# A mixture-of-experts block whose expert tiles are scattered with adding transfers instead of gathered at the end

## The reference

```
logits = x @ router_w + router_b
topv, topi = jax.lax.top_k(logits, 2)
topw = jax.nn.softmax(topv, axis=-1)
comb = einsum('bsk,bske->bse', topw, onehot)
h1 = einsum('bsd,edf->ebsf', x, W1) + b1[:, None, None, :]
h2 = einsum('bsd,edf->ebsf', x, W2) + b2[:, None, None, :]
h = h2 * jax.nn.silu(h1)
eo = einsum('ebsf,efd->ebsd', h, W3) + b3[:, None, None, :]
return einsum('bse,ebsd->bsd', comb, eo)
```

## Time and profile before

| what | value |
|---|---|
| median of three runs | 258.11 us (257.36 to 258.13) |
| profiled execution, its own time | 257.8 us |
| its span | 255.9 us |
| attentions, up to the last transpose of `xm` | 0 to 139 us |
| routing | 139 to 158 us |
| expert loop | 160 to 224 us |
| final gathers, sum and norm | 224 to 256 us |
| PE busy, DVE busy, POOL busy | 72%, 71%, 47% |

### The profile page before, as it was taken

How to read it: one execution, slowest core, us unless ns; L and a number is a source line. 1 busy time by engine, 2 the same in 40 slices (tenths; PEclk the granted TensorE clock), 3 DMA queues, 4 the chain that set the end, 5 groups by cost and what they waited for, 6 DMA issues and landing times. The chain is left out here.

```text
span 255.9 us, 7235 instructions
## 1 busy us (share of the span) xinstructions
PE 183.2 (72%) x2412; PEld 161.5 (63%) x2413; DVE 182.7 (71%) x428; ACT 118.8 (46%) x385; POOL 119.5 (47%) x220
## 2 busy tenths in 40 slices
PE   0477999999999998988774421899999999900000
PEld 0365878788887877777563421899998999900000
DVE  6406799999999999989973496277676777705344
ACT  2344868878788777676242110244454544400000
POOL 0315346655688778744225203445453341047771
PEclk9997999999999999999998555599999999975555
DMA  7699900000008000000001000011112232011212
GB/s 229 147 352 385 289 16 4 3 1 5 1 3 235 18 3 3 1 13 14 23 14 31 0 0 21 23 42 41 62 52 50 41 62 41 21 41 51 51 41 82
DMA packets 21337, 16.06 MB, mean 63 GB/s; under 512 B 3032, under 2 KB 18464, under 8 KB 21312
## 3 DMA queue, kind: packets, MB, share of 16 engines
q1 hardware_dynamic: 19248, 12.02, 16.0%
q0 software_dynamic: 1344, 2.76, 5.2%
q10 hardware_dynamic: 720, 0.95, 1.2%
HBM read 11.78 MB, written 3.93 MB: 61 GB/s over the span
## 5 line engine op out<-in xcount | busy, mean ns | idle before, releaser
L476 POOL DMA_INDIRECT early<-xm_scratch,tok_i x26 | 26.3, 1012 | 44.2 <-DMA early<-xm_scratch,tok_i 26.7
L898 DVE TENSOR_REDUCE smax<-score 128x16 f32<-128x1024 f32 x24 | 29.0, 1209 | 11.9 <-PE score L551 11.9
L384 POOL TENSOR_TENSOR k<-kt,cst 128x512 f32<-128x512 f32 x24 | 25.3, 1054 | 16.4 <-ACT kt L772 16.4
L905 DVE TENSOR_TENSOR s_sb<-score,smax 128x1024 f32<-128x1024 f32 x24 | 29.4, 1224 | 1.6 <-PE bank L499 0.8
L782 ACT ACTIVATE pt_sb<-bank 128x512 f32<-128x512 f32 x48 | 26.2, 594 | 9.3 <-PE bank L499 8.8
L551 PE MATMUL score<-k,q 64*128 64x256 f32 x192 | 26.3, 393 | 0.0
L499 PE MATMUL bank<-cst,s_sb 128*128 128x128 f32 x192 | 25.9, 279 | 0.0
L915 DVE RECIPROCAL rsum<-bank 128x128 f32<-128x128 f32 x24 | 22.8, 951 | 2.4 <-PE bank L584 2.4
L499 PEld LDWEIGHTS bank<-cst,s_sb 128*128 128x128 f32 x192 | 22.1, 144 | 0.8 <-issue 0.7
L702 PE MATMUL bank<-w,pt_sb 128*128 x160 | 22.2, 282 | 0.0
L691 PE MATMUL score<-xgt,w_now 128*128 128x128 f32 x160 | 21.4, 291 | 0.4 <-ACT xgt L854 0.4
(11 more groups left out here) (167 smaller groups left out, 383.8 us busy)
## 6 DMA issues: line engine op xcount, KB each, us to landing
w_up<-in_L_ffn_W SPq DMA_DIRECT2D x2, 2048.0 KB, 12.1
w<-in_L_ffn_W SPq DMA_DIRECT2D x8, 256.0 KB, 6.5
y_scratch<-eo SPq DMA_DIRECT2D x1, 1536.0 KB, 7.7
y_scratch<-eo SPq DMA_DIRECT2D x10, 128.0 KB
cst<-in_consts ACTq DMA_DIRECT2D x1, 672.5 KB, 4.2
early<-in_x SPq DMA_DIRECT2D x1, 512.0 KB, 6.0
early<-in_ctx SPq DMA_DIRECT2D x1, 512.0 KB, 4.3
xm_scratch<-xm SPq DMA_DIRECT2D x8, 64.0 KB, 1.5
```

The lines of the kernel that those rows point to most:

```text
L384: g.tensor_tensor(k2[:, n % 3, :, :, :], kt[:, n % 2, :].rearrange("c (b u k) -> c b u k", b=2, u=1).to_broadcast([P, 2, NQ, S]), mask_p.r ...
L476: pool.indirect_dma_start(xg[:, j, :], None, xm_d[:, :], bass.IndirectOffsetOnAxis(ap=tok_i[:, j:j + 1], axis=0)).then_inc(g_gather, 16)
L898: v.tensor_reduce(smax[:, :, :], score[:, :, :].rearrange("q b (p k) -> q b p k", k=S), AX.X, ALU.max).then_inc(d_mx, 1)
L905: v.tensor_tensor(s_sb[:, :, :].rearrange("q b (p k) -> q (b p) k", k=S), score[:, :, :].rearrange("q b (p k) -> q (b p) k", k=S), smax[:, ...
```

## The change

The gate weights move ahead of the scatter. DVE splits the weights of the two experts into three bf16 parts, multiplies them with the one-hot matrix (`hi_g`), and PE turns them round with 16 more matmuls, so that each slot has its weight (`g_slot`). `keep_out` multiplies by it. The destination of a slot is its token's row (`row_i`), and a spare row per partition for an empty slot. POOL scatters each tile with an indirect DMA that adds into one of two tables, the even tile of a pair into `y_scratch_a`, which starts as `base`, the odd one into `y_scratch_b`, which starts as zero. A scatter waits until the one before it into the same table has landed. The first seven pairs are scattered by unrolled code between the gathers; the others by a loop of POOL, whose sources are two reused tiles (`eo_last`, `row_now`), and DVE waits before it overwrites them. At the end SP reads both tables in plain order, and DVE adds the two.

The core of the diff (new code of the same lines left out):

```diff
+SURE = NT - 1
+NE_KEPT = 2 * SURE - 1
...
-            sp.wait_ge(y_zero, 16)
+            sp.wait_ge(c_base, NT)
+            sp.dma_start(y_d[0][0:SPARE, :].rearrange("(t q) e -> q t e", q=P), base[:, :, :]).then_inc(y_zero, 16)
+
             sp.wait_ge(d_ex, 1)
             last = sp.value_load(last_i[0:1, 0:1], min_val=NT - 1, max_val=NJ // 2 - 1)
-            with sp.Fori(0, last + 1) as i:
-                sp.wait_ge(d_eo, 2 * i + 2)
-                sp.dma_start(y_d.rearrange("(a q) e -> q a e", q=P)[:, bass.ds(i * 2, 2), :],
-                             eo[:, bass.ds(i * 2, 2), :]).then_inc(y_out_s, 16)
+            sp.wait_ge(y_zero, 64)
+            sp.wait_ge(g_sc[0], last * 16 + 16)
+            for h in range(2):
+                sp.dma_start(yg[:, 4 * h:4 * h + 4, :], y_row[0][:, 4 * h:4 * h + 4, :]).then_inc(in_ya, 16)
+            sp.wait_ge(g_sc[1], last * 16 + 16)
+            for t in range(NT):
+                sp.dma_start(yg[:, NT + t, :], y_row[1][:, t, :]).then_inc(g_yg[t], 16)
...
+            def scatter(u, idx, src):
+                pool.indirect_dma_start(y_d[u][:, :], bass.IndirectOffsetOnAxis(ap=idx, axis=0), src, None,
+                                        compute_op=ALU.add).then_inc(g_sc[u], 16)
+
+            for i in range(4):
+                gather(i)
+            pool.wait_ge(d_row, 2)
+            pool.wait_ge(y_zero, 64)
+            for i in range(SURE):
+                gather(i + 4)
+                for u in range(2):
+                    j = 2 * i + u
+                    pool.wait_ge(d_eo, j + 1)
+                    if i >= 1:
+                        pool.wait_ge(g_sc[u], 16 * i)
+                    scatter(u, row_i[:, j:j + 1], eo[:, j, :] if j < NE_KEPT else eo_last[:, u, :])
+            for i in range(SURE + 4, NG // 2):
+                gather(i)
...
-            for t in range(NT):
-                for k in range(2):
-                    pool.indirect_dma_start(yg[:, 2 * t + k, :], None, y_d[:, :],
-                                            bass.IndirectOffsetOnAxis(ap=slot_i[:, k, t:t + 1], axis=0)).then_inc(g_yg[t], 16)
-            last_scale(0, NT - 1)
-            last_scale(NT - 1, NT)
+            all_done()
+            with pool.Fori(SURE, last + 1) as i:
+                for u in range(2):
+                    pool.wait_ge(g_sc[u], 16 * i)
+                    pool.wait_ge(g_all, 2 * i + u + 1 - 2 * SURE)
+                    pool.wait_ge(d_eo, 2 * i + 1 + u)
+                    all_done()
+                    pool.wait_ge(y_zero, 64)
+                    scatter(u, row_now[:, u:u + 1], eo_last[:, u, :])
+            for k in range(3):
+                last_scale(k, 3 * k, min(3 * k + 3, NT))
...
+            gates = rv[:, 5:7, :].rearrange("q k t -> q (k t)")
+            link(v.tensor_copy(gate_p[:, 0, :], gates))
...
+            v.tensor_tensor(hi_g[:, :, :, :], hi_hot[:, :, :].rearrange("q c (u j) -> q c u j", u=1).to_broadcast(part),
+                            gate_p[:, :, :].rearrange("q r (c u) -> q c r u", u=1).to_broadcast(part),
+                            ALU.mult).then_inc(d_gp, 1)
...
                 hidden(1, 8 * i + 12)
+                if not kept:
+                    dve.wait_ge(g_sc[0], 16 * i + 16)
+                    last_row(0, 2 * i + 2)
                 dve.wait_ge(pe_e, 2 * i + 3)
-                keep_out(0, 2 * i + 2)
+                if kept:
+                    keep_out(0, 2 * i + 2)
+                else:
+                    keep_last(0, 2 * i + 2)
                 dve.wait_ge(d_hh, 8 * i + 16)
                 load_up(1, eb)
+            with dve.Fori(0, SURE - 1) as i:
+                turn_of(i, True)
+            with dve.Fori(SURE - 1, last) as i:
+                turn_of(i, False)
...
+            for t in range(NT + 2):
+                if t < NT:
+                    add_up(t)
+                if 1 <= t <= NT:
+                    spread(t - 1)
+                if t >= 2:
+                    mean_var(t - 2)
+                if t == NT:
+                    normalise(0)
+            for t in range(1, NT):
+                normalise(t)
```

More of the change, by code:

```diff
@@ L56 @@
 C_ORD = C_T + 2 * NT
-C_END = C_ORD + NE
+C_U = C_ORD + NE
+C_END = C_U + 1
+SPARE = NT * P
 def decoder_kernel(nc, t_in, consts, out):
@@ L168, in decoder_kernel @@
         tok_i = sb("tok_i", [P, NG], I32)
+        spare = sb("spare", [P, NG])
+        row_now = sb("row_now", [P, 2], I32)
+        row_i = sb("row_i", [P, NG], I32)
+        gate_r = sb("gate_r", [P, 2, 2 * NT])
+        gate_p = sb("gate_p", [P, 3, 2 * NT], BF16)
+        hi_g = sb("hi_g", [P, 2 * NT, 3, NG], BF16)
+        g_slot = sb("g_slot", [P, NG])
         xs = sb("xs", [P, 2, P])
@@ L252, in decoder_kernel @@
         y_zero = sem("y_zero")
-        y_out_s = sem("y_out_s")
+        g_sc = [sem("g_sc_a"), sem("g_sc_b")]
+        in_ya = sem("in_ya")
+        d_gate = sem("d_gate")
+        d_gp = sem("d_gp")
+        pe_gate = sem("pe_gate")
+        d_row = sem("d_row")
+        d_sum = sem("d_sum")
         g_all = sem("g_all")
@@ L267, in decoder_kernel @@
         d_fin = sem("d_fin")
[L269 to L270 removed]
+        xm_d = nc.dram_tensor("xm_scratch", (NT * P + 1, D), F32, kind="Internal").ap()
+        y_d = [nc.dram_tensor("y_scratch_" + k, (SPARE + P, D), F32, kind="Internal").ap() for k in "ab"]
         block = ctx.enter_context(nc.Block())
@@ L474, in _, with gather @@
             pool.wait_ge(d_tok, 1)
[L475 to L479, removed]
+            def gather(i):
+                if i >= 1:
+                    pool.wait_ge(g_gather, 32 * i)
+                for j in (2 * i, 2 * i + 1):
+                    pool.indirect_dma_start(xg[:, j, :], None, xm_d[:, :],
+                                            bass.IndirectOffsetOnAxis(ap=tok_i[:, j:j + 1], axis=0)).then_inc(g_gather, 16)
@@ L675, in _ @@
             k.then_inc(pe_tok, 1)
+            ps_gate = bank[6][:, 0:3 * NG]
+            pe.wait_ge(d_gp, 1)
+            for c in range(2 * NT):
+                k = mm(ps_gate, lo_hot[:, c, :], hi_g[:, c, :, :].rearrange("q r j -> q (r j)"),
+                       start=(c == 0), stop=(c == 2 * NT - 1))
+            k.then_inc(pe_gate, 1)
             ps_h1, ps_h2 = [bank[0], bank[2]], [bank[1], bank[3]]
@@ L1124, in keep_out, with last_row, keep_last @@
                 v.tensor_scalar(eo[:, bass.ds(j, 1), :].rearrange("q a e -> q (a e)"), ps_e[u][:, 0:D],
-                                0.0, None, ALU.add).then_inc(d_eo, 1)
+                                g_slot[:, bass.ds(j, 1)], None, ALU.mult).then_inc(d_eo, 1)
+            def last_row(u, j):
+                v.tensor_copy(row_now[:, u:u + 1], row_i[:, bass.ds(j, 1)]).then_inc(d_row, 1)
+            def keep_last(u, j):
+                v.tensor_scalar(eo_last[:, u, :], ps_e[u][:, 0:D], g_slot[:, bass.ds(j, 1)], None,
+                                ALU.mult).then_inc(d_eo, 1)
             dve.wait_ge(in_moe, MOE_LOADS)
@@ L1134, in _ @@
             take_slots(0)
+            slot_rows()
+            slot_gates()
+            dve.wait_ge(d_gate, 1)
             dve.wait_ge(g_gather, 64)
@@ L1150, in _, with turn_of @@
             keep_out(0, 0)
-            with dve.Fori(0, last) as i:
+            def turn_of(i, kept):
                 ea, eb = pair_of(i + 2)
@@ new lines, in add_up, with spread, mean_var @@
+            def add_up(t):
+                dve.wait_ge(in_ya, 16 * (t // 4 + 1))
+                dve.wait_ge(g_yg[t], 16)
+                v.tensor_tensor(acc[:, t, :], yg[:, t, :], yg[:, NT + t, :], ALU.add).then_inc(d_sum, 1)
+            def spread(t):
+                dve.wait_ge(d_sum, t + 1)
+                v.bn_stats(fstats[:, t, :], acc[:, t, :]).then_inc(d_st, 1)
+            def mean_var(t):
+                dve.wait_ge(d_st, 2 * NT + t + 1)
+                v.bn_aggr(fmv[:, t, :], fstats[:, t, :]).then_inc(d_fmv, 1)
@@ L1197, in _ @@
-            for n in range(NT // 2, NT):
-                normalise(n)
+            for t in range(NT + 2):
[9 more added lines that the diff above has]
+                normalise(t)
 def _consts():
```

71 lines of the change are left out of this document (41 added, 30 removed).

## The result

| what | before | after |
|---|---|---|
| median of four runs each, same chip | 257.88 us | 262.29 us (261.4 to 263.49) |
| ratio, 95% interval | | 1.0177 [1.0132, 1.0222] |
| span of the profiled execution | 255.9 | 261.5 (its own time 263.49) |
| first loop turn's `xs` | 170.94 | 172.06 |
| `xs` of turns 6, 7, 8 | 207.23, 213.09, 218.89 | 210.25, 223.16, 235.77 |

The forecast was 256.7, faster. The time lies inside the range and on the wrong side. A disturbed execution (one of the four of experiment 3's second kernel took 297.70 us) is left out of every ratio.

A forecast was written before the change was run, and what follows sets the result against it. It took the 31.7 us tail, 20 of them POOL making gather descriptors, behind a loop with PE and DVE nearly full; -12.3 + 1.3 + 0.8 + 6.3 + 2.5 = -1.4 gave 256.7 us, range 253.5 to 259.5 (250 to 264 with the cases).

The forecast's parts named there:

- 1.9 in hand: Expert loop: the scatter of tile 13 could end at 209.5, its output allows 211.4, so POOL has 1.9 us spare.
- The forecast's second case: POOL becomes the bound: an adding transfer costs it 1.31, not 0.95; 260.6 us, chance 0.21.
- The tail: Behind E, the end of the last expert tile: 31.7 us become 19.4, 12.3 shorter, bounds 10.5 to 14.
- The start: Before the loop: five linked DVE steps and `hi_g` make `xs` 1.3 us later, bounds 0.6 to 2.4.
- The loop: Expert turns: added copies cost 0.8 us in all, bounds 0 to 2; POOL's four transfers, 5.25 a turn, keep up.
- The wait in turn 7: DVE waits before filling tile 16 until the scatter of tile 14 has landed: 6.3 us, bounds 3.5 to 10.
- The clock: PE idles 5.1 us in the turn-7 wait, its clock falls: 2.5 us more, bounds 0 to 2.6.
- the first case: Short stall: the turn-7 wait is 4.1, PE idles 2.9, under the clock's 3.2, so no clock loss; 252.0 us, chance 0.24.
- The slow landing: An adding write lands in 3.15, not 2.2, costing 0.95 in stall and tail each: 258.6 us; in the forecast's 0.45.
- copies hold POOL's descriptors back: Fourth case: DVE's copies block POOL, 6.5 us a turn, scatter of tile 13 5.4 late; 262.1 us, chance 0.07.

The follow-up runs named there:

- experiment 3's second kernel: Changed kernel with all ten pairs scattered by unrolled code from tiles of their own, gathers of pairs 11 and 12 behind the last scatter: 253.06 us, ratio 0.9842.
- experiment 1: Changed kernel with plain scatters that overwrite instead of adding: 261.08 us in a single execution.
- The gates alone: Kernel before with only the gate part: weights turned round to the slots and multiplied in at the copy out of PSUM: 259.35 us, ratio 1.0064.
- experiment 6: Plain scatters on the changed kernel with trailing gathers moved (254.49 us); gates, gathers ahead, or both on the kernel before (254.47 to 259.35 us).
- timed six-pairs-ahead kernel: Kernel before with the gathers of the first six pairs fired one behind another, two gather semaphores: 255.55 us, ratio 0.9993.
- the one with gates: Kernel before with gates computed per slot and six pairs gathered ahead: 258.62 us, ratio 1.0106.
- experiment 4: Changed kernel, turn 6 without its two waits; gathers of pairs 11 and 12 between scatters 15 and 16 (258.41 us), or behind POOL's loop (253.68 us).
- experiment 2: Changed kernel with the gathers of pairs 11 and 12 moved behind POOL's loop: 254.86 us, ratio 0.9912.
- first kernel of experiment 3: Changed kernel with all ten pairs scattered by unrolled code from tiles of their own, so no tile is reused: 254.65 us, ratio 0.9912.
- plain scatters: Changed kernel with overwriting instead of adding scatters and the gathers of pairs 11 and 12 behind POOL's loop: 254.49 us, ratio 0.990.
- experiment 5: Changed kernel with more gathers ahead, two semaphores: seven pairs, no tile reuse, trailing gathers moved (262.22 us); six pairs, none trailing (259.33 us).
- second kernel of experiment 5: Changed kernel with six pairs gathered ahead without waiting for each landing, one more pair per turn, none trailing: 259.33 us, ratio 1.0054.
- first kernel of experiment 5: Changed kernel without tile reuse, gathers of pairs 11 and 12 behind the last scatter, seven pairs gathered ahead: 262.22 us, ratio 1.0217.

## Why the prediction was wrong

**The failed step** is in the paragraph on the loop: "POOL now issues four transfers per turn: 4 x (1.012 + 0.30) = 5.25 us by the mean of its gathers", and "POOL has 1.9 in hand". It took the price of a gather for an adding scatter. The scatter measured 1.66 in the mean, 1.56 with DVE idle (the one at 245.12), and without the addition 1.00 (experiment 1). So POOL had nothing in hand: its scatter of tile 13 ended at 221.38 (219.80 + 1.58) and not at 211.4. The 10.0 us are made up like this. At tile 1 POOL was 2.9 late already (180.88 for 178.0), 1.8 of it because the gathers of pair 4 started at 174.90 and not at 173.08. Its six turns took 6.75 each and not 5.25, 9.0 in all, 7.8 of it from twelve scatters at 0.65 over the mean that was taken and the rest from gathers at 1.10. The 1.9 in hand goes off that. The forecast's second case named this and its threshold, 0.14 us more per scatter, gave it a chance of 0.21, and priced it by the slowest gather, 0.36 more. With 0.65 its formula gives 14 x 0.65 - 1.9 = 7.2, beside the 5.13 + 2.26 = 7.4 of turn 6. That the two agree so well is in part luck: DVE waited there for tiles 11 and 12, and the formula leaves out the late start. The mechanism of the case was right and its size nearly a factor of two low. Its sign, scatters above 1.1 us with POOL never idle, was the one that showed. No row showed an adding write, and then the bound belongs farther out than the slowest row of another kind.

Point by point:

- *The tail, -12.3*: measured -13.5, right. Inside it two errors cancel in part. The first sum on DVE started at E + 7.8 and not 5.8, because the last scatter stood behind that of tile 18 (243.18 + 1.55) and then took 1.56. What follows took 10.4 and not 13.6: DVE takes a tile in 0.49 and not 0.85, since its three small instructions start 0.1 to 0.2 apart and their rows overlap.
- *The start, +1.3*: measured 1.1, right; `hi_g` took 1.46.
- *The loop, +0.8*: 1.9, too low and in bounds. It is two longer turns, 7.9 and 6.8 in turns 1 and 4; the kernel before has two as well (6.5 and 6.8 in turns 1 and 3). The gates alone (experiment 6) put E 1.65 later, with 2.1 from turn 0 to turn 8, and beside the timed six-pairs-ahead kernel the one with gates has turns of 5.97 for 5.83. But the kernels of experiment 4 have the weights too (copies of 0.34 instead of 0.28) and turns of 5.8. What makes single turns longer was not found.
- *The wait in turn 7, +6.3*: 6.68, the turn 6.8 longer. Shown by experiment 2, which took it away. Its parts were off by the backlog twice: tile 14 landed 16.5 after tile 13 was out, not 14.2, and DVE came to it 9.9 after and not 8.0, so that the wait came out near the forecast by luck in part.
- *The clock, +2.5*: 2.2, and the same thing in turn 6, inside its 7.05. The 3.2 us that the first case leaned on is no fixed time: the clock fell about 2.1 and 4.7 after PE's two stops.
- *Missing: the wait in turn 6, +7.05.* It is the whole miss: -1.4 + 7.05 gives 5.65, measured 5.6; the errors of the other terms, -1.2 to +1.1 each, cancel.
- *The rivals.* The short stall did not happen. POOL as the bound is what came. The slow landing did not: a scatter into `y_scratch_a` took 3.7 from issue to landing, 2.1 of it behind the generation. That copies hold POOL's descriptors back is not what made the scatters slow: with DVE idle the transfer at 245.12 took 1.56, beside copies the mean was 1.66, and the slowest of all runs 2.15 (222.31 in the first kernel of experiment 3). It is the rule of the Trainium skill, page "SBUF — State Buffer", section "SBUF: two separate sides" (the "DVE blocks DMA" trap). By that rule nearly each of two copies a turn would have added 0.7; the traces show scatters at most 0.6 above the 1.56, and 0.1 in the mean of the changed kernel.

DMA packets show what the addition changes: the queue of POOL's transfers moved 1,344 packets before, 1,472 in experiment 1 and 3,712 in the changed kernel. 2,240 more than in experiment 1, for 20 scatters, is 112 each:

```profile
q0 software_dynamic: 3712, 3.02, 9.3%
```

**What stays open**: the holds in experiments 1, 3, 5 and 6, in which PE, ACT and DVE stand with "issue" or "remote" (ACT's idle rows there are up to 7.2 long, ordinary waits included), and which make the first turn up to 12 us late or single turns up to 5 us longer. Shown is where they are not from: not from dense gathers, not from the gates, not from the addition (experiment 1 and plain scatters have them), and not from register loads, since ACT's copy at 171.24 follows none. All kernels that show them have scatters in POOL's program and the longer code that goes with it, but the kernels of experiment 4 have both and had turns of 5.8, and in experiment 5 the hold begins before the first scatter. That the engines' own instructions arrive late would fit, but the profile does not bear it out: the two queues named "instruction" moved 16 or 17 and 9 or 10 packets in every run, with holds or without, and none from 162 to 176 us in the second kernel of experiment 5. No run isolates the cause.

## What to carry to other kernels

Moving work from the tail into the loop pays only if the engine that gets it has the time, counted with the price of the very instruction: an adding indirect transfer cost GpSimd 1.6 us per 128 rows of 512 bytes, and a plain one 1.0. When an engine is behind and its turn is no shorter than the others', look for the first place where another one waits on it; a wait removed there comes back at the next true dependency (the 5.73 and 2.29 of experiment 2 became 8.18 in experiment 4), and what helps is less work ahead of the transfer that is waited for. And look at what stands in a queue ahead of the instruction that somebody waits for: four gathers of unused tiles cost 7 us here, and moving them behind the loop turned a loss of 1.8% into a gain of 0.9%, for inputs that don't use those tiles.

## What was not expected of the hardware

- An adding scatter has some 144 packets and a plain one 32 (112 less), and the engine time follows: 1.6 for 1.0.
- A plain scatter took 1.18 to 1.25 where it ran beside DVE's copy, once a turn at the same place (experiment 1), and 1.00 elsewhere. The delay by DVE is small against the transfer's own length.
- DVE's addition, statistics and variance of a tile, 0.29, 0.29 and 0.17 in the rows, took 0.49 a tile when interleaved over tiles.
- PE can halt within a product whose operands are all there, for 0.35 (plain scatters) to 1.03 us (first kernel of experiment 5).
